# The low part of one product: from a GpSimd subtraction to an adding DMA

## The chip, the core and the metric

The kernel runs on one core of a Trainium2 chip. The metric is the device time of one execution in microseconds (us). Five engines work side by side, each in its own order of instructions, and wait for one another only through semaphores: TensorE (PE in the profile; PEld is its weight load), VectorE (DVE), ScalarE (ACT), GpSimd (POOL) and SyncE (SP, which here only issues DMAs). Sixteen DMA engines move the data.

## The reference

A recommendation model: 32 embedding rows of 64 numbers per sample are looked up, a two-layer "compressed interaction network" is computed on them, and three small dense layers follow. What takes the time is the two interaction layers; all numbers are float32.

```
e   = stack([tbl_f[ids[:, f]] for f in 32 fields], axis=1)        # (1024, 32, 64)
z0  = einsum('bhd,bmd->bhmd', e, e).reshape(batch, 32*32, 64)
o0  = relu(einsum('bcd,oc->bod', z0, W0) + b0)                    # 128 outputs
h   = o0[:, :64]                                                  # 64 go on, 64 are summed
z1  = einsum('bhd,bmd->bhmd', h, e).reshape(batch, 64*32, 64)
o1  = relu(einsum('bcd,oc->bod', z1, W1) + b1)                    # 128 outputs
y   = mlp(concat([sum_d(o0[:, 64:]), sum_d(o1), dense]))
```

## The kernel before, in words

The batch is cut into 128 steps (STEPS) of 8 samples, which give 512 columns (SC = 8 samples x 64 dimensions). In the code m is the step. Fields lie along the 128 partitions. In each step the second layer needs 16 tiles of 128 partitions x 512 columns of products h x e; VectorE makes them in four buffers: p1 (prod[1], 4 tiles), p2 (prod[2], 4 tiles), p3 (prod[3], 4 tiles) and twice 2 tiles in the PSUM buffer z4. A fifth product, prod[0], belongs to the first layer of the next step.

TensorE multiplies plain float32 slowly and a rounded form (float32r) fast. So 14 of the 16 second-layer tiles are split in two: ScalarE writes the rounded part zh (`round_split`, line 372), and somebody writes the rest, zl = product - zh, also in the rounded form. TensorE then makes three fast products for each tile, W1h x zh, W1l x zh and W1h x zl (`split`, line 625). The five parts u are: 0 (4 tiles of p1), 1 (4 tiles of p2), 2 (the first 2 tiles of p3), 3 and 4 (2 tiles each, from z4). The other 2 tiles of p3 go in whole (`whole`, line 616). The low part zl is made by GpSimd for u = 0, 1, 2 (`low_part`, line 217) and by VectorE for u = 3, 4 (`low_part4`, line 512).

The order on each engine is written out by hand, and semaphores of one count per step tie them together. In step m:

- TensorE: split(m-1, 1), split(m-1, 4), split(m-1, 2); first layer of step m+1 (lines 609 and 611); split(m, 3), split(m, 0), the whole tiles. So part 2 of step m is used in TensorE's turn m+1, right ahead of the first layer of step m+2.
- ScalarE: copy_x; in even steps copy_left, in odd ones round_left; round_split 0 and 3; finish_l1(m-1) (line 378), which reads the finished second layer of step m-1 and so waits for split(m-1, 2); round_split 1 and 4; replicate_h0(m+1) (line 385), which waits for the first layer of step m+1; finish_l0(m+1) (line 402); round_split 2; replicate_h1(m+1) (line 385).
- VectorE: product 0 of step m+1, low_part4(m-1, 1), p1, z4, p2, low_part4(m, 0), z4 again, p3, the sum of the second layer of step m-1; every second step three small operations more. The first z4 waits for replicate_h1, low_part4(m, 0) for round_split 3.
- GpSimd: two gathers of embedding rows (line 200), low_part 0, 1, 2, in odd steps the row numbers (line 196).
- SyncE issues all other loads: rot_low for step m+4 and rot_high for step m+2 (1 MB each, line 269), replicated rows, and the write of gathered rows to DRAM (line 259). DMAs issued by GpSimd go to a queue of their own (q0 in the profile), SyncE's to q1.

The semaphores around the change: zh_made[2] is raised by ScalarE's rounding of part 2, zl_made[2] by GpSimd's subtraction; TensorE's split waits for zl_made, and VectorE waits for zl_made[2] of the step before ahead of writing p3 again.

Of the kernel before, what the change touches and what calls it, by code (L numbers as in the profile page):

```python
# [5 lines left out]
F32 = mybir.dt.float32  # L6
F32R = mybir.dt.float32r
I32 = mybir.dt.int32
ALU = mybir.AluOpType
ACT = mybir.ActivationFunctionType  # L10
# [48 lines left out]
SIZES = (4, 4, 2, 2, 2)  # L59
# [6 lines left out]
def cin_mlp(nc, ids, first_row, tables, dense_t, w0_first, w0_second, w0l_first, w0l_second, w1, b0, b1,  # L66
            w_top1, b_top1, w_top2, b_top2, w_top3, y):
    ctx = ExitStack()
    with ctx:
# [6 lines left out]
        def sem(name):  # L76
            return ctx.enter_context(nc.semaphore(name))
# [53 lines left out]
        gather_started = sem("gather_started")  # L131
# [19 lines left out]
        p1_made = sem("p1_made")  # L151
        p2_made = sem("p2_made")
        p3_made = sem("p3_made")
        z4_made = [sem(f"z4_made{k}") for k in range(2)]
        zh_made = [sem(f"zh_made{u}") for u in range(PARTS)]
        zl_made = [sem(f"zl_made{u}") for u in range(PARTS)]
# [32 lines left out]
        def is_up_to(i, c, m):  # L189
            return not known(i) or BODY * i + c <= m  # L190

        @block.gpsimd
        def _(pool):

            def number_rows(n, b):
                pool.tensor_tensor(idx[b][:, :], ids_sb[:, bass.ds(n * GATHERS, GATHERS)], first_row_sb[:, :],  # L196
                                   ALU.add).then_inc(idx_made, 1)

            def gather(b, g):
                pool.indirect_dma_start(  # L200
                    out=emb[b][:, g, :], out_offset=None, in_=tables,
                    in_offset=bass.IndirectOffsetOnAxis(ap=idx[b][:, g:g + 1], axis=0),
                ).then_inc(gathered[b], 16)

            def gathers(i, c):
                n, b = i * 2 + c // 2 + AHEAD, (c // 2 + AHEAD) % 2
                if c % 2 == 0:
                    pool.wait_ge(idx_made, n + 1)
                    pool.sem_inc(gather_started, 1)
                for g in range(c % 2 * 2, c % 2 * 2 + 2):  # L210
                    gather(b, g)

            def low_part(m, u, product):
                pool.wait_ge(zh_made[u], m + 1)
                if not known(m) or m > 0:
                    pool.wait_ge(split_used[u], m)
                pool.tensor_tensor(zl[u][:, :, :], product[:, 0:SIZES[u], :], zh[u][:, :, :].bitcast(F32),  # L217
                                   ALU.subtract).then_inc(zl_made[u], 1)

            def step(i, c):  # L220
                m = i * BODY + c
                if is_up_to(i, c, LAST - 2 * AHEAD):
                    gathers(i, c)
                low_part(m, 0, prod[1])
                low_part(m, 1, prod[2])
                low_part(m, 2, prod[3])
                if c % 2 and is_up_to(i, c, LAST - 2 * AHEAD - 2):
                    n, b = i * 2 + c // 2 + AHEAD + 1, (c // 2 + AHEAD + 1) % 2
                    pool.wait_ge(scratch_written[b], (i + (c // 2 + AHEAD + 1) // 2) * WRITTEN)
                    number_rows(n, b)  # L230

            pool.wait_ge(ids_loaded, 32)
            for n in range(AHEAD):
                if n >= 2:
                    pool.wait_ge(scratch_written[n % 2], WRITTEN)
                number_rows(n, n % 2)
                pool.wait_ge(idx_made, n + 1)
                for g in range(GATHERS):
                    gather(n % 2, g)
            pool.wait_ge(scratch_written[AHEAD % 2], AHEAD // 2 * WRITTEN)  # L240
            number_rows(AHEAD, AHEAD % 2)
            for c in range(BODY):
                step(0, c)
            with pool.Fori(1, ITERS - 2) as i:
                for c in range(BODY):
                    step(i, c)
            for k in (ITERS - 2, ITERS - 1):
                for c in range(BODY):
                    step(k, c)
# [97 lines left out]
        def _(act):  # L347
# [20 lines left out]
            def round_split(m, u, made, product):  # L368
                act.wait_ge(made, m + 1)
                if not known(m) or m > 0:  # L370
                    act.wait_ge(split_used[u], m)
                act.activation(zh[u][:, :, :], product, ACT.Copy).then_inc(zh_made[u], 1)  # L372
# [32 lines left out]
            def step(i, c):  # L405
                m = i * BODY + c
                b = c % HALVES
                if is_up_to(i, c, LAST - 2):
                    copy_x(m + 2, b)
                if b == 0 and is_up_to(i, c, LAST - 2):  # L410
                    copy_left(i * 2 + (c + 2) // 2)
                if b == 1 and is_up_to(i, c, LAST - 1):
                    round_left(i * 2 + (c + 1) // 2)
                round_split(m, 0, p1_made, prod[1][:, :, :])
                round_split(m, 3, z4_made[0], z4[:, :, :])
                if is_past(i, c, 0):
                    finish_l1(m - 1)
                round_split(m, 1, p2_made, prod[2][:, :, :])
                round_split(m, 4, z4_made[1], z4[:, :, :])
                if is_up_to(i, c, LAST - 1):  # L420
                    replicate_h0(m + 1)
                    finish_l0(m + 1, 1 - b, i * 2 + (c + 1) // 2)
                round_split(m, 2, p3_made, prod[3][:, 0:SIZES[2], :])
                if is_up_to(i, c, LAST - 1):
                    replicate_h1(m + 1)

# [58 lines left out]
        def _(dve):  # L485
# [41 lines left out]
            def step(i, c):  # L527
                m = i * BODY + c
                b = c % HALVES
                later = not known(m) or m > 0  # L530
                low = rot_low[c]
                high = rot_high[b]
                if is_up_to(i, c, LAST - 1):
                    products_l0(m + 1, (c + 1) % 4, i + (c + 1) // 4 + 1)
                if later:
                    low_part4(m - 1, 1)
                if b == 1 and is_up_to(i, c, LAST - 1):
                    left_products(i * 2 + (c + 1) // 2)
                dve.wait_ge(hrep0_made, m + 1)
                if later:  # L540
                    dve.wait_ge(zl_made[0], m)
                nc.vector.tensor_tensor(prod[1][:, :, :], repeated(hrep[0], LOW), low[:, :, :],  # L542
                                        ALU.mult).then_inc(p1_made, 1)
                if b == 1 and is_up_to(i, c, LAST - 1):
                    left_low(i * 2 + (c + 1) // 2)
                dve.wait_ge(hrep1_made, m + 1)
                if later:
                    dve.wait_ge(zl_made[4], m)
                nc.vector.tensor_tensor(z4[:, :, :], repeated(hrep[1], 2), low[:, 0:2, :],  # L549
                                        ALU.mult).then_inc(z4_made[0], 1)  # L550
                if b == 1:
                    sum_l0(i * 2 + c // 2)
                dve.wait_ge(rot_high_loaded[b], (i * 2 + c // 2 + 1) * (16 * QUADS))
                if later:
                    dve.wait_ge(zl_made[1], m)
                nc.vector.tensor_tensor(prod[2][:, :, :], repeated(hrep[0], LOW), high[:, :, :],  # L556
                                        ALU.mult).then_inc(p2_made, 1)
                low_part4(m, 0)
                dve.wait_ge(zl_made[3], m + 1)
                nc.vector.tensor_tensor(z4[:, :, :], repeated(hrep[1], 2), low[:, 2:4, :],  # L560
                                        ALU.mult).then_inc(z4_made[1], 1)
                if later:
                    dve.wait_ge(zl_made[2], m)
                    dve.wait_ge(whole3_used, m)
                nc.vector.tensor_tensor(prod[3][:, :, :], repeated(hrep[1], LOW), high[:, :, :],  # L565
                                        ALU.mult).then_inc(p3_made, 1)
                if later:
                    sum_l1(m - 1)
# [32 lines left out]
        def _(pe):  # L601
# [16 lines left out]
                mm.then_inc(used, 1)  # L618

            def split(m, u, start=False, stop=False):  # L620
                pe.wait_ge(zl_made[u], m + 1)
                for t in range(SIZES[u]):
                    k = FIRST[u] + t
                    for part, (w, z) in enumerate(((w1h, zh[u]), (w1l, zh[u]), (w1h, zl[u]))):
                        mm = nc.tensor.matmul(out1[:, :], w[:, k, :], z[:, t, :], start=start and t == 0 and part == 0,  # L625
                                              stop=stop and t == SIZES[u] - 1 and part == 2)
                mm.then_inc(split_used[u], 1)
# [116 lines left out]
```

## Time and profile before

| What | us |
|---|---|
| Median of 3 runs (lowest, highest) | 2021.87 (2021.35, 2022.53) |
| The profiled execution, its own time | 2021.81 |
| Its span in the trace | 2020.0 |
| TensorE busy with matmuls | 1967.9 |
| VectorE busy | 1931.2 |
| GpSimd busy | 1731.4 |
| ScalarE busy | 1679.0 |

The span runs from the first to the last instruction of the trace; the execution's own time holds 1.8 us more. An engine is busy while one of its computing instructions runs; waiting and issuing DMAs don't count. Shares of busy time are means over the whole span; the start and the end take some 85 us, and the rest is the loop of steps, which repeats every two steps.

### The profile page before, as it was taken

To read this page: it belongs to the slowest core of one execution; us is meant where nothing else is said; L and a number is where in the kernel's file an instruction comes from. 1 tells how busy PE (TensorE), PEld (TensorE's weight loads), DVE (VectorE), ACT (ScalarE), POOL (GpSimd) and SP (SyncE) were. 2 spreads that over 40 slices of the span, in tenths; PEclk is the share of its full clock that TensorE was granted. 3 is DMA by queue.
4 is the path that set the end of the run, shared out by engine and by line. 5 is a ranking of instruction groups with operands and counts; after the bars stand their busy time and mean duration, and the time that the engine had idled before them with its cause. 6 is when DMAs were issued, how large, how long until landed. Compare 5 with 4: busy or idle time off the path is not lost.

```text
span 2020.0 us, 28616 instructions
## 1 busy us (share of the span) xinstructions
PE 1967.9 (97%) x7112; PEld 1333.8 (66%) x7112; DVE 1931.2 (96%) x1356; ACT 1679.0 (83%) x1943; POOL 1731.4 (86%) x708
## 2 busy tenths in 40 slices
PE   2999999999999999999999999999999999999998
PEld 0666666666666666666666666666666666666664
DVE  3999999999999999999999999999999999999991
ACT  2888888888888888888888888888888888888883
POOL 3998998998998998998988988988988989988871
PEclk9999999999999999999999999999999999999999
DMA  7998788788788788788888887887888887887820
GB/s 188 207 212 205 176 189 193 177 190 192 178 189 191 181 188 190 182 189 187 184 187 187 185 190 183 186 188 184 187 189 182 188 190 180 190 189 179 190 67 1
DMA packets 268306, 364.14 MB, mean 180 GB/s; under 512 B 107506, under 2 KB 107890, under 8 KB 268163
## 3 DMA queue, kind: packets, MB, share of 16 engines
q1 hardware_dynamic: 258338, 352.61, 77.1%
q0 software_dynamic: 8192, 8.40, 1.5%
q10 hardware_dynamic: 1760, 2.96, 0.5%
q8 instruction: 6, 0.10, 0.0%
q14 instruction: 10, 0.07, 0.0%
HBM read 347.02 MB, written 16.78 MB: 180 GB/s over the span
## 4 chain that ended last, share of the span: by engine, by line
PE 94%; POOL 3%; SPq 1%; issue 1%; DMA 1%; ACT 0%; DVE 0%; POOLq 0%
PE out L625 60%; PE out L609 21%; PE out L616 10%; POOL zl L217 2%; PE out L611 1%; POOL emb L200 1%; SPq L259 0%; PE out L673 0%; DMA fields_dram<-emb 0%; PE hrep L673 0%; SPq L284 0%; SPq L269 0%; DMA first_row_sb<-in_first_row 0%; PE out L666 0%; PE z L666 0%
## 5 line engine op out<-in xcount | busy, mean ns | idle before, releaser
L217 POOL TENSOR_TENSOR zl<-prod,zh 128x2048 fp32r<-128x2048 f32 (+1 forms) x384 | 1476.1, 3869 | 120.5 <-ACT zh L372 69.3
L372 ACT ACTIVATE zh<-prod 128x2048 fp32r<-128x2048 f32 (+1 forms) x384 | 626.2, 1631 | 183.3 <-DVE prod L556 79.0
L625 PE MATMUL out<-zh,w1h 128*128 128x512 f32 x1792 | 745.7, 416 | 11.1 <-DVE zl L512 5.0
L625 PE MATMUL out<-zl,w1h 128*128 128x512 f32 x1792 | 700.4, 391 | 0.0
L625 PE MATMUL out<-zh,w1l 128*128 128x512 f32 x1792 | 699.1, 390 | 0.0
L385 ACT ACTIVATE hrep<-out,b_sb 32x512 f32<-32x512 f32 (+1 forms) x768 | 494.7, 644 | 14.5 <-PE out L611 4.7
L609 PE MATMUL out<-prod,w_sb 128*128 128x512 f32 x1024 | 464.1, 596 | 35.6 <-DVE prod L495 30.6
L625 PEld LDWEIGHTS out<-zh,w1h 128*128 128x128 f32 x1792 | 336.8, 188 | 169.2 <-issue 55.5
L625 PEld LDWEIGHTS out<-zh,w1l 128*128 128x128 f32 x1792 | 337.3, 188 | 83.3 <-issue 16.7
L625 PEld LDWEIGHTS out<-zl,w1h 128*128 128x128 f32 x1792 | 336.7, 188 | 74.2
L609 PEld LDWEIGHTS out<-prod,w_sb 128*128 128x128 f32 x1024 | 194.8, 190 | 232.5 <-issue 222.7
L200 POOL DMA_INDIRECT emb<-in_tables,idx x256 | 244.5, 955 | 103.0 <-POOL idx L196 50.5
L512 DVE TENSOR_TENSOR zl<-z,zh 128x1024 fp32r<-128x1024 f32 x256 | 310.5, 1213 | 6.5 <-ACT zh L372 6.5
L372 ACT ACTIVATE zh<-z 128x1024 fp32r<-128x1024 f32 x256 | 261.6, 1022 | 65.4 <-DVE z L560 60.7
L495 DVE TENSOR_TENSOR prod<-xr,rot_low 128x2048 f32<-128x2048 f32 x128 | 291.9, 2280 | 19.9 <-DMA rot_low<-fields_dram 15.8
L565 DVE TENSOR_TENSOR prod<-hrep,rot_high 128x2048 f32<-128x2048 f32 x128 | 291.8, 2280 | 0.0
L556 DVE TENSOR_TENSOR prod<-hrep,rot_high 128x2048 f32<-128x2048 f32 x128 | 291.8, 2280 | 0.0
L542 DVE TENSOR_TENSOR prod<-hrep,rot_low 128x2048 f32<-128x2048 f32 x128 | 291.8, 2279 | 0.0
L616 PE MATMUL out<-prod,w_sb 128*128 128x512 f32 x512 | 240.3, 591 | 0.0
L560 DVE TENSOR_TENSOR z<-hrep,rot_low 128x1024 f32<-128x1024 f32 x128 | 157.8, 1232 | 4.4
L549 DVE TENSOR_TENSOR z<-hrep,rot_low 128x1024 f32<-128x1024 f32 x128 | 157.0, 1227 | 2.8 <-ACT hrep L385 0.8
L616 PEld LDWEIGHTS out<-prod,w_sb 128*128 128x128 f32 x512 | 96.3, 188 | 71.5 <-issue 61.6
(52 smaller groups left out, 751.1 us busy)
## 6 DMA issues: line engine op xcount, KB each, us to landing
rot_low<-fields_dram SPq DMA_DIRECT2D x512, 256.0 KB
rot_high<-fields_dram SPq DMA_DIRECT2D x512, 256.0 KB
xrep<-fields_dram SPq DMA_DIRECT2D x256, 128.0 KB
fields_dram<-emb SPq DMA_DIRECT2D x512, 32.0 KB
left_x<-fields_dram SPq DMA_DIRECT2D x256, 64.0 KB
left_y<-fields_dram SPq DMA_DIRECT2D x256, 64.0 KB
emb<-in_tables,idx POOLq DMA_INDIRECT x256
w_sb<-in_w ACTq DMA_DIRECT2D x1, 1024.0 KB
```

The costliest lines, as they stand in the source:

```text
L200: pool.indirect_dma_start(out=emb[b][:, g, :], out_offset=None, in_=tables, in_offset=bass.IndirectOffsetOnAxis(ap=idx[b][:, g:g + 1], axi ...
L217: pool.tensor_tensor(zl[u][:, :, :], product[:, 0:SIZES[u], :], zh[u][:, :, :].bitcast(F32), ALU.subtract).then_inc(zl_made[u], 1)
L372: act.activation(zh[u][:, :, :], product, ACT.Copy).then_inc(zh_made[u], 1)
L385: op = act.activation(hrep[j][to, :], out0[h, :], ACT.Relu, bias=b0_sb[h, :])
L495: nc.vector.tensor_tensor(prod[0][:, :, :], repeated(xr, LOW), rot_low[c][:, :, :], ALU.mult).then_inc(x_made, 1)
L512: nc.vector.tensor_tensor(zl[3 + k][:, :, :], z4[:, :, :], zh[3 + k][:, :, :].bitcast(F32), ALU.subtract).then_inc(zl_made[3 + k], 1)
L542: nc.vector.tensor_tensor(prod[1][:, :, :], repeated(hrep[0], LOW), low[:, :, :], ALU.mult).then_inc(p1_made, 1)
L556: nc.vector.tensor_tensor(prod[2][:, :, :], repeated(hrep[0], LOW), high[:, :, :], ALU.mult).then_inc(p2_made, 1)
L565: nc.vector.tensor_tensor(prod[3][:, :, :], repeated(hrep[1], LOW), high[:, :, :], ALU.mult).then_inc(p3_made, 1)
L609: nc.tensor.matmul(out0[:, :], w0_sb[:, t, :], prod[0][:, t, :], start=t == 0, stop=False)
L616: mm = nc.tensor.matmul(out1[:, :], w1_sb[:, tiles.start + t, :], product[:, t, :], start=False, stop=False)
L625: mm = nc.tensor.matmul(out1[:, :], w[:, k, :], z[:, t, :], start=start and t == 0 and part == 0, stop=stop and t == SIZES[u] - 1 and part ...
```

## The change

ScalarE writes minus the rounded part into zl[2], directly after it has written the rounded part. GpSimd then issues one DMA from prod[3] to zl[2] that adds (`accum_op=ALU.add`) and so leaves product - rounded part there: 128 partitions of 4 KB, 0.524 MB. Its subtraction of part 2 is gone. Two semaphores are new: low3_filled (ScalarE to GpSimd, the fill is written) and low3_loaded (the DMA has landed), for which TensorE and VectorE now wait where they waited for zl_made[2].

```diff
                 low_part(m, 0, prod[1])
                 low_part(m, 1, prod[2])
-                low_part(m, 2, prod[3])
+                pool.wait_ge(low3_filled, m + 1)
+                pool.sem_inc(gather_started, 1)
+                pool.dma_start(zl[2][:, :, :].bitcast(F32), prod[3][:, 0:SIZES[2], :],
+                               accum_op=ALU.add).then_inc(low3_loaded, 16)
...
                 round_split(m, 2, p3_made, prod[3][:, 0:SIZES[2], :])
+                act.wait_ge(zh_made[2], m + 1)
+                act.activation(zl[2][:, :, :], zh[2][:, :, :].bitcast(F32), ACT.Copy, scale=-1.0).then_inc(low3_filled, 1)
                 if is_up_to(i, c, LAST - 1):
                     replicate_h1(m + 1)
...
                 if later:
-                    dve.wait_ge(zl_made[2], m)
+                    dve.wait_ge(low3_loaded, m * 16)
                     dve.wait_ge(whole3_used, m)
...
             def split(m, u, start=False, stop=False):
-                pe.wait_ge(zl_made[u], m + 1)
+                if u == 2:
+                    pe.wait_ge(low3_loaded, m * 16 + 16)
+                else:
+                    pe.wait_ge(zl_made[u], m + 1)
```

## Rows read from the trace of the kernel before

**Rows 1.** Busy time by window (start:end): PE, PEld, DVE, ACT, POOL; clock; DMA.
```profile
1000.55:1030.79 30.24, 30.18 (x112) 20.61 (x111) 30.08 (x21) 25.99 (x31) 27.03 (x12) 1.00 0.82 186
500.00:1500.00 1000.00, 997.32 (x3641) 681.73 (x3640) 994.63 (x695) 859.69 (x993) 893.30 (x365) 1.00 0.82 187
```

**Rows 2.** Waits, whole run: total us, times, longest.
```profile
PEld out L625 <- POOL zl L217: 45.1, 120, 1.4
```

**Rows 3.** Chain of waits, one step: start us, duration us, what.
```profile
1002.25 3.43 PE out L609 x8
1005.68 0.23 PE out L611
1005.98 4.34 PE out L625 x18
1010.32 1.72 PE out L616 x4
1012.04 5.49 PE out L625 x24
```

**Rows 4.** Timeline of ScalarE, one step: start us, duration us, instruction.
```profile
1007.13 1.03 ACT L372 ACTIVATE zh<-z 128x1024 fp32r<-128x1024 f32 x1 [0.48 <-DVE z L560]
1008.06 1.30 ACT L385 ACTIVATE hrep<-out,b_sb 64x512 f32<-64x512 f32 x2
1009.38 0.69 ACT L402 ACTIVATE relu<-out,b_sb 64x512 f32<-64x512 f32 x1
1010.09 1.06 ACT L372 ACTIVATE zh<-prod 128x1024 fp32r<-128x1024 f32 x1
1011.18 2.62 ACT L385 ACTIVATE hrep<-out,b_sb 32x512 f32<-32x512 f32 x4
1013.82 0.60 ACT L354 ACTIVATE xr<-xrep 128x512 f32<-128x512 f32 x1
1014.36 0.59 ACT L360 ACTIVATE lz<-left_x 128x512 f32<-128x512 f32 x1
1015.44 1.92 ACT L372 ACTIVATE zh<-prod 128x2048 fp32r<-128x2048 f32 x1 [0.50 <-issue]
1017.26 1.00 ACT L372 ACTIVATE zh<-z 128x1024 fp32r<-128x1024 f32 x1
1018.16 0.68 ACT L378 ACTIVATE relu<-out,b_sb 128x512 f32<-128x512 f32 x1
1018.77 1.91 ACT L372 ACTIVATE zh<-prod 128x2048 fp32r<-128x2048 f32 x1
```

**Rows 5.** Timeline of VectorE, columns as in rows 4.
```profile
1005.87 1.23 DVE L560 TENSOR_TENSOR z<-hrep,rot_low 128x1024 f32<-128x1024 f32 x1
1018.65 1.21 DVE L512 TENSOR_TENSOR zl<-z,zh 128x1024 fp32r<-128x1024 f32 x1
```

**Rows 6.** Groups by line and shape: busy us, mean ns, idle before.
```profile
L217 POOL TENSOR_TENSOR zl<-prod,zh 128x2048 fp32r<-128x2048 f32 x256 | 1173.8, 4597 | 120.5 <-ACT zh L372 69.3 <-issue 51.0
L217 POOL TENSOR_TENSOR zl<-prod,zh 128x1024 fp32r<-128x1024 f32 x128 | 308.7, 2412 | 0.0
```

**Rows 7.** Timeline of GpSimd in the loop.
```profile
1006.73 6.98 POOL L217 TENSOR_TENSOR zl<-prod,zh 128x2048 fp32r<-128x2048 f32 x2 [0.34 <-ACT zh L372]
```

**Rows 8.** Timelines of GpSimd and SyncE's queue at the start.
```profile
9.81 0.94 POOL L200 DMA_INDIRECT emb<-in_tables,idx  x1 [0.30 <-issue]
12.26 5.16 SPq L259 DMA_DIRECT2D fields_dram<-emb  x8
```

**Rows 9.** Busy time by window, columns as in rows 1.
```profile
6.00:7.00 1.00, 0.00 (x0) 0.00 (x0) 0.94 (x4) 0.00 (x0) 0.86 (x1) 1.00 0.98 401
1006.00:1008.00 2.00, 2.00 (x9) 1.66 (x10) 2.00 (x2) 1.52 (x2) 1.67 (x2) 1.00 0.12 35
1012.00:1014.00 2.00, 2.00 (x11) 1.60 (x10) 2.00 (x3) 1.95 (x4) 1.86 (x2) 1.00 1.07 234
```

**Rows 10.** Timeline of TensorE after an idle time, and the window behind it.
```profile
41.72 2.68 PE L609 MATMUL out<-prod,w_sb 128*128 128x512 f32 x3 [4.96 <-ACT hrep L385]
42.00:44.00 2.00, 2.00 (x3) 0.66 (x2) 2.00 (x2) 0.00 (x0) 1.42 (x2) 0.50 1.09 246
```

More of the change, by code:

```diff
@@ L153, in cin_mlp @@
         p3_made = sem("p3_made")
+        low3_filled = sem("low3_filled")
+        low3_loaded = sem("low3_loaded")
         z4_made = [sem(f"z4_made{k}") for k in range(2)]
```

## The prediction

> **What bounds the kernel now.** I read first how busy each engine is in the steady loop. Two steps take 30.24 us, 15.12 a step, and in them TensorE works 30.18 us and VectorE 30.08 [rows 1]; over 1000 us the picture is the same (997 and 995). So two engines are full at once. GpSimd has 27.03 of 30.24 and ScalarE 25.99. Second I read the chain of waits: it stays on TensorE through a whole step, its pieces following each other with at most 0.07 us between [rows 3]. Third the waits: the weight loads waited 45.1 us in 120 times for GpSimd's low parts [rows 2], 0.4 us each. But weight loads run ahead of the matmuls, and the matmuls themselves stand still for only 0.06 us in two steps [rows 1]. The reader should see that taking work from GpSimd can give back almost nothing: if both TensorE's and VectorE's gaps closed, at most 30.24 - 30.08 = 0.16 us for two steps, 10 us in 64 pairs. What the change adds to latency and to ScalarE is the question.
>
> **What it removes.** 128 GpSimd subtractions of 2.41 us [rows 6]. The larger ones, 4.60 us each, are the last thing TensorE needs from GpSimd, for part 1; they are gated by ScalarE's rounding, not by the small one: such a pair starts after GpSimd had run dry for 0.34 us [rows 7]. Gain on the path: 0.
>
> **What it adds to ScalarE.** One pass over 128x1024, SBUF to SBUF. Its nearest row is the rounding of the same shape ahead of it, 1.06 us, next instruction 1.09 later [rows 4]; it waits for that rounding's own semaphore, for which I add 0.05. I take 1.15 us; bounds 0.95 (the step from round to next for the PSUM form, 1007.13 to 1008.06 = 0.93) and 1.3. Queued behind it are replicate_h1, the copies, and round_split 0 and 3. Only 0.49 us of idle stands between the copies' end (1014.36 + 0.59 = 1014.95) and round_split 0 (1015.44), so rounding 3 ends 1.15 - 0.49 = 0.66 us later, at 1018.26 + 0.66 = 1018.92 [rows 4]. VectorE begins its low part of that very result at 1018.65 [rows 5]: it would wait 0.27, with the hand-over about 0.3 us. VectorE has no idle time to win it back. In the other step of the pair VectorE comes to that point later, having three small operations more, so the price is 0.3 us a pair, 64 x 0.3 = 19 us. This alone would give 2021.8 + 19 = 2041. GpSimd's issue (a gather's took 0.94 us [rows 8]) replaces 2.41 us of work; GpSimd stays below its bound.
>
> **What it adds as latency.** Before, part 2 was ready 2.4 us after GpSimd got to it. Now it is fill, issue, transfer, landing. TensorE meets part 2 right ahead of the first layer, and ScalarE makes the next fill only behind that first layer's result. That closes a loop through one step, and I add it up from the end E of split(m, 2):
> - first layer of step m+2: 3.43 + 0.23 = 3.66 us [rows 3];
> - ScalarE: in the same time finish_l1, round_split 1 and 4 (0.61 + 1.91 + 0.93, about 3.5 us from E, so level with the 3.66); then replicate_h0 to the start of replicate_h1, 1011.18 - 1008.06 = 3.12 us, in which round_split 2 of step m+1 is made [rows 4];
> - the fill: 1.15 us;
> - GpSimd issues, the data land: L, counted from the start of the issue;
> - split(m+1, 2): 6 of the 24 matmuls of a 5.49 us piece = 1.37 us [rows 3];
> - three hand-overs between engines at about 0.08 us (VectorE to ScalarE took 0.03, 1007.10 to 1007.13 [rows 4, 5]; a longer one is my estimate for PE and the DMA): 0.25.
>
> Sum 3.66 + 3.12 + 1.15 + 1.37 + 0.25 = 9.55 us, plus L. Before, that loop had GpSimd's 2.4 and no fill, 10.8 of 15.12: harmless. Now it takes the period over as soon as L is above 15.12 - 9.55 = 5.57 us. Below that TensorE merely runs somewhat later against VectorE and nothing is lost. GpSimd's order is no hindrance: it ends low part 1 some 4.6 us after ScalarE's rounding 1 (2.6 us behind E), at E + 7.2, before the fill is there at E + 7.9.
>
> **How long is L?** No row shows an adding DMA, nor any 0.5 MB transfer from GpSimd. Fixed part: a 32 KB gather issued at 9.81 was landed when SyncE went on at 12.26, with the DMAs nearly idle: 2.45 us [rows 8]. Moving part: 0.524 MB. At the best rate in the trace, 401 GB/s for long rows [rows 9], counted once, 1.31 us: L = 3.76, the lower bound. But an add must read the target too, so I count 1.05 MB; and it starts some 8 us behind E, when SyncE has just issued 2 MB of rotations, in a burst where the DMAs are full at 234 GB/s [rows 9]. If the added queue gets as much as the burst carries, 234 GB/s, that is 4.5 us: L = 2.45 + 4.5 = 6.95. If it gets half of it, 9.0 us: L = 11.4, the upper bound. I take L = 7.0, since the transfer does lie in the burst but its 4 KB rows are longer than the loads' 2 KB.
>
> A price that only pages have: the Trainium skill, "DMA: Bandwidth & Descriptors", section "Anatomy of one DMA — SWDGE (gpsimd) path", fits one such transfer by about 2.0 us + bytes/436e3. By it L would be 3.2 us and the loop harmless. "Collectives: The Full Stack", "The bandwidth ceiling: the fold count and why AG ≠ RS ≠ AR", speaks against it: adding halves the rate because two sources are read, not because of the sum. No run here shows either.
>
> **The sum.** Period 9.55 + 7.0 = 16.55 us, 1.43 more than 15.12. Over 127 steps 182 us on the profiled execution's own 2021.8 (the median is 0.06 away): 2203 us. ScalarE's 0.3 us vanish in it, since VectorE then has slack. I cost TensorE's clock at nothing: it is 1.00 through the loop [rows 1]. It fell to 0.50, the 1.2 GHz level, after 4.96 us without work [rows 10]; here the stalls are near 1.5 us a step.
>
> **The rivals.**
> - A. The transfer is in time (L below 5.57) and only ScalarE's pass shows: 2041 us. For it: a lower bound of 3.76 and long rows. Against it: the burst. The skill's fit named above would lead here. Chance 0.14.
> - B. The DMA engines fill up. In two steps they are busy 0.82 of 30.24 = 24.8 us [rows 1]; two transfers of 4.5 us make 33.8, or 16.9 a step: 2021.8 + 127 x 1.78 = 2248, near the forecast by another way; at half the rate, with L = 11.4, the period is 20.95 and the time 2762. For it: bursts already run full. Against: in between (1006 to 1008) the share is 0.12 [rows 9]. Chance of a time above 2450 for either reason: 0.15.
> - C. Not slower: the transfer is in time and ScalarE's pass fits as well. The place is VectorE's low part at 1018.65: it decides at a pass of 0.49 + 0.35 = 0.84 us and L below 5.57. Then 2022 us, or down to 2012 with the gaps of the first paragraph closed. Against it: every row of that shape is near 1 us. Chance 0.10.
> - The forecast, a loop with L between 5.57 and about 8.9 (2022 to 2450 us): 0.61.
>
> **The numbers.** A measurement of this kernel can tell 0.2%, about 4 us. All but rival C is slower: 0.90; within 0.2% 0.07, faster 0.03. The range is 2018 to 2450: it takes in A and C nearly whole and the loop up to L = (2450 - 2022)/127 + 5.57 = 8.9, and leaves about 0.17 out, nearly all above.
>
> **What would show it.** In the changed kernel the weight loads of line 625 wait for the DMA zl<-prod once per step, and the chain of waits goes TensorE, ScalarE, DMA, TensorE, with a period near 16.5 us; VectorE shows idle time ahead of z4, waiting for line 385. From GpSimd's DMA to TensorE's next split should be 7 us. The chain still all on TensorE, with VectorE waiting some 0.3 us for the rounding in every second step, would mean A. A DMA share near 1 without quiet windows would mean B. TensorE's clock under 1.00 in the loop would make all of it wrong, upwards.

## The result, and the profile after

| | us |
|---|---|
| Before, median of 4 runs | 2021.8 (2021.4 to 2022.5) |
| Changed, median of 4 runs | 2469.7 (2467.7 to 2480.2) |
| Ratio | 1.2227, 95% interval 1.2201 to 1.2253 |
| Predicted | 2203, range 2018 to 2450 |

The change costs 448 us, 7.0 us for each of the 64 pairs of steps: a pair now takes 37.2 us in place of 30.24. The way was right; the time lies 20 us above the range, and the forecast had only 40% of the loss. The profiled execution is the longest of the four (2480.2 us, span 2478.3). Of all executions here one of the two of the control e8 was disturbed, at a clock of 0.75 and 2850.6 us, and is left out.

The first view is the page of the changed kernel: the busy times, TensorE's granted clock in 40 slices, and the DMA queues (packets, MB, share of 16 engines).

```profile
PE 2145.2 (87%) x7112; PEld 1426.2 (58%) x7112; DVE 1951.1 (79%) x1356; ACT 1812.3 (73%) x2071; POOL 1569.8 (63%) x708
PEclk9998988989989989889889889889899889899899
q1 hardware_dynamic: 258338, 352.61, 61.8%
q0 software_dynamic: 26624, 75.52, 15.8%
```

VectorE's busy time is nearly the old one in a longer span, so it now waits. TensorE has the same 7112 matmuls and is busy 177 us longer: it runs slower, which the clock row, mostly 8 and 9, hints at. The loop's window answers to [rows 1] (columns as there):

```profile
500.00:1500.00 1000.00, 878.87 (x2925) 588.32 (x2926) 807.18 (x559) 745.93 (x850) 652.84 (x292) 0.91 0.80 178
```

No engine is full now, and neither are the DMAs. What is waited for is in the view of the waits, beside [rows 2]:

```profile
ACT relu L383 <- PE out L635: 375.4, 128, 6.4
PE out L635 <- DMA zl<-prod: 285.3, 67, 5.5
POOL zl L230 <- ACT zl L430: 255.1, 122, 3.0
DVE prod L502 <- PE out L618: 233.1, 64, 4.0
DVE left_parts L512 <- ACT left_parts L371: 107.3, 64, 1.7
```

TensorE's matmuls stood still for the adding DMA 285 us in 67 waits (the loop has 64 pairs): in every second step only, 4.3 us each. The chain of waits through one pair, without its smallest pieces, shows the loop (start us, duration us, what):

```profile
1195.94 1.23 DVE z L556
...
1197.89 2.20 DVE prod L563
1200.09 1.14 DVE zl L519
1201.26 1.24 DVE z L567
...
1204.78 0.69 ACT relu L407
1205.49 1.07 ACT zh L377
1206.58 1.06 ACT zl L430
...
1208.23 8.34 DMA zl<-prod
1216.62 2.93 PE out L635 x6
1219.55 4.98 PE out L616 x8
...
1232.26 0.52 ACT left_parts L371
...
1233.53 1.23 DVE z L556
```

From the issue at 1208.23 the data take 8.34 us. Then TensorE makes part 2 in 2.93 us, where six of the 24 matmuls took 1.37, and the first layer in 4.98 where it took 3.43 [rows 3]. ScalarE goes on, and the next fill is there at 1229; but that step's DMA is not on the chain. The chain leaves the even step over round_left, VectorE's small subtraction and z4, and comes to the next odd step's DMA. The reason for the slow matmuls is in the windows of two us (columns as in rows 1; the number before the last two is the clock):

```profile
1212.00:1214.00 2.00, 0.10 (x1) 0.00 (x0) 2.00 (x1) 2.00 (x2) 1.26 (x2) 1.00 1.17 226
1214.00:1216.00 2.00, 0.00 (x0) 0.00 (x0) 1.90 (x3) 0.16 (x1) 2.00 (x1) 0.92 1.03 206
1216.00:1218.00 2.00, 1.38 (x3) 1.16 (x4) 2.00 (x2) 0.00 (x0) 1.86 (x1) 0.50 0.40 91
1220.00:1222.00 2.00, 2.00 (x4) 0.78 (x3) 0.69 (x1) 2.00 (x3) 0.00 (x0) 0.50 1.06 258
1224.00:1226.00 2.00, 2.00 (x10) 1.46 (x9) 1.15 (x1) 1.20 (x2) 2.00 (x1) 1.00 1.06 230
```

After 4.5 us without a matmul TensorE comes back at 0.50 of full speed, its 1.2 GHz level, and has 1.00 again only at about 1224. (1.56 + 1.55 =) 3.1 us are lost to it in this pair.

Where the 8.34 us go is in the queues' packets (queue: packets, MB, share of 16 engines). From 1210 to 1212, two to four us after the issue, only SyncE's queue moves anything, its rotation loads:

```profile
q1 hardware_dynamic: 255, 0.46, 107.2%
```

From 1214 to 1216 nearly all traffic is the adding DMA's own:

```profile
q0 software_dynamic: 119, 0.37, 89.3%
q1 hardware_dynamic: 177, 0.04, 13.6%
```

So the transfer isn't slowed by the burst so much as held back by it. The trace records every packet; medians over steps 9 to 117, counted from the issue, are these. In odd steps the first packet of the adding DMA starts after 4.5 us, when all but a few packets of the rotation loads are through, the last one ends after 7.9, and the landing is at 8.3. In even steps, where SyncE's loads are through before the issue, they are 1.5, 4.4 and 4.7 us. The same transfer is 3.6 us later in odd steps, and 2.9 of them pass before its first packet.

### The profile page after: what moved, and what is told of

It is laid out like the page before. It is cut to its first block, busy times and chain, and to the rows that moved or that the text cites. A ratio compares the mean times of both kernels' runs of the same rounds, so it can differ in the third digit from the quotient of the medians.

```text
span 2478.3 us, 28985 instructions
## 1 busy us (share of the span) xinstructions
PE 2145.2 (87%) x7112; PEld 1426.2 (58%) x7112; DVE 1951.1 (79%) x1356; ACT 1812.3 (73%) x2071; POOL 1569.8 (63%) x708
## 3 DMA queue, kind: packets, MB, share of 16 engines
q0 software_dynamic: 26624, 75.52, 15.8%
## 4 chain that ended last, share of the span: by engine, by line
PE 23%; DMA 23%; ACT 22%; DVE 16%; issue 14%; SPq 1%; DVEq 0%; POOL 0%; POOLq 0%; ACTq 0%
DMA zl<-prod 22%; PE out L616 13%; PE out L635 8%; ACT hrep L390 7%; ACT zh L377 6%; DVE prod L563 5%; ACT relu L407 3%; ACT zl L430 3%; DVE z L567 3%; DVE z L556 3%; DVE zl L519 3%; DVE sums L524 2%; ACT xr L359 1%; ACT left_parts L371 1%; PE out L618 1%
## 5 line engine op out<-in xcount | busy, mean ns | idle before, releaser
L219 POOL TENSOR_TENSOR zl<-prod,zh 128x2048 fp32r<-128x2048 f32 x256 | 1171.2, 4575 | 461.2 <-ACT zh L377 461.2
L635 PE MATMUL out<-zh,w1h 128*128 128x512 f32 x1792 | 794.5, 443 | 292.0 <-DMA zl<-prod 285.3
L635 PE MATMUL out<-zl,w1h 128*128 128x512 f32 x1792 | 731.3, 408 | 0.0
L635 PE MATMUL out<-zh,w1l 128*128 128x512 f32 x1792 | 730.0, 407 | 0.0
L616 PE MATMUL out<-prod,w_sb 128*128 128x512 f32 x1024 | 556.6, 694 | 35.7 <-DVE prod L502 30.7
L635 PEld LDWEIGHTS out<-zh,w1l 128*128 128x128 f32 x1792 | 355.6, 198 | 99.3 <-issue 30.4
L616 PEld LDWEIGHTS out<-prod,w_sb 128*128 128x128 f32 x1024 | 238.2, 233 | 297.8 <-issue 280.8
L383 ACT ACTIVATE relu<-out,b_sb 128x512 f32<-128x512 f32 x128 | 87.9, 687 | 375.4 <-PE out L635 375.4
L230 POOL DMA_DIRECT2D zl<-prod x128 | 124.4, 972 | 269.4 <-ACT zl L430 255.1
L623 PE MATMUL out<-prod,w_sb 128*128 128x512 f32 x512 | 240.3, 591 | 0.0
L530 DVE TENSOR_REDUCE feat<-relu 128x512 f32 (+1 forms) x128 | 87.2, 681 | 98.7 <-ACT relu L383 98.7
```

The costliest lines, as they stand in the source:

```text
L616: nc.tensor.matmul(out0[:, :], w0_sb[:, t, :], prod[0][:, t, :], start=t == 0, stop=False)
L623: mm = nc.tensor.matmul(out1[:, :], w1_sb[:, tiles.start + t, :], product[:, t, :], start=False, stop=False)
```

## The experiments

Three theories stood against each other: the DMA's time to landing closes a loop (the prediction's), with the clock on top; ScalarE's pass costs; the DMAs' traffic costs. Intervals are those of the ratio to the kernel before; "landing" is read from the chain of waits, in odd steps, of which the fences show one each (start us, duration us, what).

**ScalarE's pass alone** (e1).

```diff
# the kernel before, and:
+                act.wait_ge(zh_made[2], m + 1)
+                act.activation(spare[:, :, :], zh[2][:, :, :].bitcast(F32), ACT.Copy, scale=-1.0)
```

> The kernel before, with ScalarE's extra pass of 128x1024 written into a spare tile that nobody reads; GpSimd still subtracts. Theory (the DMA's time from issue to landing closes a loop TensorE, ScalarE, DMA, TensorE; ScalarE's pass is minor): the pass delays rounding 3 in every second step by some 0.3 us, 64 x 0.3 = 19 us, so about 2041 us, at most 2050. Rival 1 (ScalarE's pass is what costs, since it sits ahead of replicate_h1 and round_left): 2200 us or more.

Measured 2035.1 us, ratio 1.0070 (1.0053 to 1.0087): 14 us, of the 19 reckoned. VectorE runs on with 992 of 1000 us busy. The pass is not what costs.

**The same arithmetic, added by GpSimd** (e2).

```diff
-                pool.dma_start(zl[2][:, :, :].bitcast(F32), prod[3][:, 0:SIZES[2], :],
-                               accum_op=ALU.add).then_inc(low3_loaded, 16)
+                pool.tensor_tensor(zl[2][:, :, :], prod[3][:, 0:SIZES[2], :], zl[2][:, :, :].bitcast(F32),
+                                   ALU.add).then_inc(low3_loaded, 16)
```

> The changed kernel, but GpSimd adds the product on to the filled tile by its own instruction (2.4 us) where the changed kernel issues the DMA; all waits as changed. Theory: the loop is 9.55 + about 2.5 = 12 us and does not bind; only ScalarE's pass shows, about 2041 us as in the run with the pass alone. Rival 1 (the pass and its wait cost): as slow as the changed kernel, near 2470. If this is 2041 and the changed kernel 2470, the DMA alone holds some 430 us.

Measured 2038.4 us, ratio 1.0090 (1.0073 to 1.0107). So 431 us of the 448 come with the DMA. GpSimd's own time is not the reason: it is busy 1733 us here against 1570 in the changed kernel. Whether the reason is the DMA's time to landing or its traffic, e4 to e12 tell.

**A plain copy** (e3; the low part is the whole product).

```diff
-                pool.dma_start(zl[2][:, :, :].bitcast(F32), prod[3][:, 0:SIZES[2], :],
-                               accum_op=ALU.add).then_inc(low3_loaded, 16)
+                pool.dma_start(zl[2][:, :, :].bitcast(F32), prod[3][:, 0:SIZES[2], :]).then_inc(low3_loaded, 16)
```

> The changed kernel, but the DMA copies the product over the filled tile instead of adding (the low part is then the whole product; same bytes written, the target not read). Theory with the adding itself costly: the time to landing falls from a median of 6.3 us by 1 to 2 us, the loop by as much, and TensorE's idle times get short enough for its clock to stay up: 2150 to 2300 us. Rival 2 (an add costs what a copy costs; waiting behind the other queue's traffic and the fixed time are what is long): within 30 us of 2470.

Measured 2352.5 us, ratio 1.1640 (1.1621 to 1.1660), 50 us above the expected band but far from the rival. The landing is near 7.0 us in odd steps, 1.3 less than adding, and 2.9 in even ones, where adding takes 4.7:

```profile
1218.54 7.09 DMA zl<-prod
1225.68 2.93 PE out L634 x6
1228.61 5.06 PE out L615 x8
```

TensorE's clock falls here too, so little of its loss comes back. What adding costs the DMA engines is in the queue's share: 

```profile
q0 software_dynamic: 26624, 75.52, 9.0%
```

9.0% of 16 engines over 2350.6 us is 3385 us; the gathers' part is 1.8% of 2035.7 x 16 = 586 (in e2, where the queue has them alone); the rest over 128 x 16 is 1.37 us a transfer and engine. For adding it is 15.8% of 2478.3 x 16 less the same, 2.77 us. Twice the time for the same bytes: 0.524 MB / 2.77 us = 189 GB/s against 383. The Trainium skill ("Collectives: The Full Stack", section "The bandwidth ceiling: the fold count and why AG ≠ RS ≠ AR") says of ring collectives on several cores that the step that adds runs at about half the rate of the one that copies, because an add reads two sources. The ratio of 2.0 agrees with that; that the second read is the reason no run here shows.

**A small adding DMA** (e4; 64 of 1024 columns get the sum).

```diff
-                pool.dma_start(zl[2][:, :, :].bitcast(F32), prod[3][:, 0:SIZES[2], :],
+                pool.dma_start(zl[2][:, 0, 0:64].bitcast(F32), prod[3][:, 0, 0:64],
```

> The changed kernel, but the adding DMA covers 64 of the 1024 columns (32 KB in place of 512 KB; the rest of the low part stays minus the rounded part). Theory (moving bytes is most of the time to landing): landing at about 2.5 to 3.5 us as the gather at the start of the trace before, loop under 13 us, so 2041 us. Rival 2 (the time is queueing behind the other queue's packets, whatever the size): landing stays at 5 us or more and the time above 2150 us.

Measured 2272.9 us, ratio 1.1243 (1.1221 to 1.1266). Here my theory failed: with a sixteenth of the bytes the landing is still near 6.1 us:

```profile
1211.06 5.93 DMA zl<-prod
1217.03 2.87 PE out L635 x6
1219.90 3.82 PE out L616 x8
```

and the queues show why. From 1214 to 1215, over three us after the issue, there is still no packet of GpSimd's queue q0:

```profile
q1 hardware_dynamic: 130, 0.23, 102.7%
```

Its packets come from 1215 to 1216:

```profile
q1 hardware_dynamic: 487, 0.16, 98.4%
q0 software_dynamic: 107, 0.03, 29.0%
```

The first starts 4.3 us after the issue in odd steps (median) and 1.5 us in even ones, as with 512 KB; the last ends 1.2 us later. Bytes are the smaller part of the landing; most of it is the wait for the first packet, and that is there for 32 KB too. The Trainium skill ("DMA: Bandwidth & Descriptors", "Queues, rings and completion order") has each DMA engine take turns between the queues that have work, a packet (there a group of descriptors) at a time, by which so small a transfer should have passed the burst early. The long start does not look like it. What follows does: from 1214 to 1215 in the changed kernel q0 and q1 have 48 packets each.

**TensorE kept busy in the stall** (e5; w_zero is a tile of zeros, so the sum is unchanged).

```diff
                     split(m - 1, 4)
+                    if c % 2 == 0:
+                        for _ in range(18):
+                            nc.tensor.matmul(out1[:, :], w_zero[:, :], w1h[:, 0:4, :], start=False, stop=False)
                     split(m - 1, 2, stop=True)
```

> The changed kernel, with 18 extra matmuls by a tile of zeros (they add nothing to the sum) in every second step, between split(m-1, 4) and split(m-1, 2), where TensorE stands still for 4.5 to 5 us until the DMA has landed. They are some 4.1 us of work at 2.4 GHz. Theory (the stall makes the clock fall to 0.50, and the matmuls behind it cost 3.1 us more in every second step: 2.93 in place of 1.37 for split 2, 4.98 in place of 3.43 for the first layer): the clock stays near 1.00 and the kernel gets faster although it does more, 64 x 3.1 = 200 us, so about 2270 us. Rival (the clock is no part of it, the landing alone is): no change, 2470, or slower by the added work.

Measured 2316.7 us, ratio 1.1455 (1.1436 to 1.1474): 153 us faster than the changed kernel, with 1152 matmuls more. The landing is what it was, the matmuls behind it are quick:

```profile
1201.29 8.20 DMA zl<-prod
1209.54 1.66 PE out L639 x6
1211.19 3.43 PE out L620 x8
```

The clock over the loop is 1.00, and a pair takes 34.8 us in the trace in place of 37.5. So at least 153 us, a third of the 448, was the clock's fall. The control, the same 18 matmuls in the kernel before (e8):

> Control for the zero matmuls: the kernel before with the same 18 in every second step. There TensorE has no idle time, so 18 x 0.228 = 4.1 us a pair should show in full: 2021 + 64 x 4.1 = 2284 us. If they cost much less, they are no measure of work.

Measured 2260.9 us in one run: 240 us, 3.7 a pair. The added matmuls are real work, which only the stall hides.

**SyncE's loads behind the landing** (e6).

```diff
                     sp.wait_ge(z4_made[1], m + 1)
+                    sp.wait_ge(low3_loaded, m * 16 + 16)
                     load_low(m + 4, c)
```

> The changed kernel, but SyncE issues a step's rotation loads and writes to DRAM only after that step's adding DMA has landed, so that it doesn't meet the burst that they make. Theory (the long landings, 8.3 us in odd steps, last until the other queue's burst is over): landing falls to the 4.7 us of the shortest ones or somewhat over, TensorE's stalls and the clock's fall go, 2040 to 2150 us. Rival (the landing time is the DMA's own): landing stays at 6 to 8 us, 2470 us or more, since loads now come later too.

Measured 2183.2 us (2166.6 to 2193.0), ratio 1.0773 (1.0725 to 1.0822), somewhat over the band. Not a byte less is moved, and 287 us are gone. The first packet starts 2.2 us after the issue, and the landing is 5.2 to 6.1 us in most odd steps:

```profile
1200.73 5.97 DMA zl<-prod
1206.75 2.21 PE out L636 x6
1208.96 4.53 PE out L617 x8
```

**A quarter of the rotation bytes in the loop** (e9).

```diff
+                few = 1 if not known(m) else LOW
-                                  ap=[[PITCH, FIELDS], [QUADS * PITCH, LOW], [1, SC]])
-                    sp.dma_start(tile[q * FIELDS:(q + 1) * FIELDS, :, :], src).then_inc(loaded, 16)
+                                  ap=[[PITCH, FIELDS], [QUADS * PITCH, few], [1, SC]])
+                    sp.dma_start(tile[q * FIELDS:(q + 1) * FIELDS, 0:few, :], src).then_inc(loaded, 16)
```

> The changed kernel, but the rotation loads inside the loop fetch one of four rows (a quarter of the bytes, the rest of the tiles keeps old values). Theory (queueing behind the burst): the DMA lands in 4.7 us or less in all steps, 2040 to 2060 us. Rival (its own time, or one-way effects of ScalarE's pass): landing above 6 us and more than 2300 us.

Measured 2131.2 us, ratio 1.0538 (1.0520 to 1.0555). The first packet starts after 1.5 us in odd steps too. The landing is steady at 5.05 us, but that is still too long; both sides' bands missed.

```profile
1198.95 5.05 DMA zl<-prod
1204.05 1.65 PE out L636 x6
1205.70 3.43 PE out L617 x8
```

The next odd DMA is issued at 1230.45 there: a pair of 31.50 us, of which 26.45 is everything but the landing. The same for e5: 34.85 - 8.25 = 26.6, taking the pair as 30.24 + (2316.7 - 2021.8)/64 and the landing's usual 8.25. So the loop is about 26.5 us plus the landing in one of two steps, and binds from a landing of 30.24 - 26.5 = 3.7 us on.

**Both small** (e12: the diffs of e4 and e9 together).

> The changed kernel with both a quarter of the rotation bytes and an adding DMA of 32 KB. With the three other cases (full and small DMA beside full loads, full DMA beside light loads) it gives the landing's parts. Theory: floor of 2.5 to 3.5 us from issue to landing; the loop 29 to 30 us, under 30.24, so only ScalarE's pass shows: 2035 to 2045 us. Rival (a fixed time over 4 us even for a small adding DMA with quiet DMAs): 2060 us or more.

Measured 2054.5 us, ratio 1.0164 (1.0147 to 1.0181), between the two bands and 16 us over e2. TensorE waited for the DMA 6 times in all, 13.4 us, of which 13.0 near the start and the end, where the loads are full; so the loop no longer binds. Most landings are missing from this trace, but the DMA's last packet ends 2.0 to 2.2 us after the issue in odd and even steps alike. A long fixed time, the rival, is not what e4 met.

**ScalarE's round_left earlier** (e10).

```diff
-                if b == 1 and is_up_to(i, c, LAST - 1):
-                    round_left(i * 2 + (c + 1) // 2)
...
                 act.activation(zl[2][:, :, :], ..., scale=-1.0).then_inc(low3_filled, 1)
+                if b == 0 and is_up_to(i, c, LAST - 2):
+                    round_left(i * 2 + (c + 2) // 2)
```

> The changed kernel, with ScalarE's round_left moved from the start of an odd step to the end of the even step before, ahead of replicate_h1 (4 copies, 2.62 us) and copy_x. Theory as it now stands (the loop runs over two steps: DMA in the odd one, TensorE, ScalarE, round_left, VectorE's small subtraction and z4, p2, ScalarE, DMA; its length is 26.3 us + the landing + the clock's loss): VectorE no longer waits 1.7 us for round_left, z4 starts when replicate_h1 ends, 1.3 us earlier than now; 64 x 1.3 = 83 us, so about 2385 us. Rival (the loop goes through one step, TensorE, ScalarE, DMA, as predicted, and VectorE isn't in it): no change, 2470.

Measured 2475.2 us, ratio 1.2251 (1.2230 to 1.2271): nothing gained. This is not the rival's one-step loop either. Its chain of waits:

```profile
1200.99 9.71 DMA zl<-prod
1210.75 2.93 PE out L635 x6
1213.67 4.82 PE out L616 x8
...
1218.73 4.13 PE out L635 x18
1222.86 1.72 PE out L623 x4
1224.57 5.49 PE out L635 x24
1230.06 3.43 PE out L616 x8
...
1238.57 9.60 DMA zl<-prod
```

round_left and VectorE are off the chain, as meant; the even step now goes through TensorE's own work. The loop without the landing fell to (37.58 - 9.71 =) 27.9 us, clock loss included, from 37.59 - 8.34 = 29.2 (z4 to z4, 1195.94 to 1233.53). But the landing grew from 8.34 to 9.71, the same 1.4 us. Why is in SyncE's order: the step's first rotation loads, in the changed kernel and here, are issued at

```profile
1202.67 1.87 SPq L274 DMA_DIRECT2D rot_low<-fields_dram  x4
1197.12 1.95 SPq L274 DMA_DIRECT2D rot_low<-fields_dram  x4
```

The adding DMA follows 5.6 us behind them there and only 3.9 here, and its first packet comes after 5.6 us (median) in place of 4.5. From these loads to the landing it is 13.9 us there and 13.6 here, and from the landing to the next odd step's rotation loads (1240.26 and 1234.33) 23.7 and 23.6. z4, which releases them, was ready at 1195.25 here, but SyncE was still issuing the loads of left_y until 1196.9. So the DMA issued earlier lands no earlier. The reader should see that an edit can be right about the path and still gain nothing, if what it brings forward then waits for something that the edit did not move.

**round_left earlier and loads behind the landing** (e11: the diffs of e6 and e10 together).

> The same together with SyncE's loads behind the landed DMA, the two changes that shorten the loop without taking away work. Theory: 2183 less up to 83 us, so 2080 to 2120 us; it stays above the kernel before, since the loop's 25 us and a landing near 6 still exceed 30.24. Rival: 2183, as with the loads alone.

Measured 2172.8 us, ratio 1.0751 (1.0733 to 1.0769): 10 us less than e6 alone, which is within the spread of e6's runs, and not the 60 to 100 forecast. The landings are 6.1 to 7.0 us in most odd steps against 5.2 to 6.1 in e6, and the first packet starts after 3.0 us in place of 2.2: as in e10, most of what the path over round_left gives is spent on a longer landing. No version here beats the kernel before: the best that keeps the DMA and all the work is this one, 151 us above it.

## Why the prediction was wrong

What bounds the kernel before: right as far as the runs go. TensorE is full: 18 matmuls more cost 3.7 us a pair (e8). That relieving GpSimd gives nothing is read from the rows; no run tests it without the other parts of the change, and no version is under 2035.

ScalarE's pass: right. 19 us forecast, 14.0 measured alone (e1), 17 with GpSimd adding (e2).

The mechanism, a loop TensorE, ScalarE, fill, DMA, TensorE that takes the period over: right in kind. From the odd DMA's issue to the even one's (1229.59 in the changed kernel's timeline of GpSimd) it took 21.36 us; the prediction's sum 9.55 with the measured landing 8.34 and the clock's 3.1 gives 21.0. One hand-over was set too short: the fill ends at 1206.58 + 1.06 = 1207.64 and GpSimd's DMA begins at 1208.23, 0.6 us later and not 0.08. But the loop was drawn through one step and taken for both alike. It binds in odd steps; the even one takes 16.2 us, held by what lies between its fill and the next odd one, with no DMA on the chain; that this is near the forecast's 16.55 is chance. For a pair the prediction had 2 x 16.55 = 33.1 us, the changed kernel 37.2.

The landing: 7.0 forecast, 8.3 measured in odd steps (8.1 to 8.6 in four of five). Mis-sized by 1.3 us in the step that counts, 64 x 1.3 = 83 us. Its makeup was wrong too. A fixed 2.45 and bytes at the burst's rate would have made e4's 32 KB land in under 3 us; it took 6.1. What holds it is the other queue's burst, shown by e6 (the same bytes, moved behind: 5.2 to 6.1) and e9 (fewer of them: 5.05), and the adding itself 1.3 (e3). The forecast had the transfer share the burst's rate for 4.5 us; in the trace it waits 2.9 us longer than in even steps for its first packet and then has the engines nearly alone, for 3.4 us. That 7.0 came near 8.3 is in part luck. The transfer should have been read against when the rotation loads ahead of it are through, not against the burst's rate.

The step that failed: "I cost TensorE's clock at nothing", with its reason "here the stalls are near 1.5 us a step". I had spread the loop's excess evenly over the steps. It comes in one stall of 4.5 us in every second step, and behind that the clock is at 0.50 for some 7 us. By the trace's matmuls 3.1 us a pair, by e5 at least 153 us of the total, 2.7 us a pair in the loop, which is the difference between 2470 and 2317. With the clock held the time lies inside the range, 114 us over the point. I had named a clock under 1.00 as what would make all of it wrong, and gave it no price and no chance, though [rows 10] showed the fall.

The rivals: A (in time, only ScalarE's pass) needed a landing under 5.57; the loop as measured needs 3.7, and even with light loads it was 5.05. C the same. B (DMA engines full) is not what happened: their share over the loop is 0.80 against 0.82, and after the burst there are windows at 0.00. The Trainium skill's fit for one transfer from GpSimd ("DMA: Bandwidth & Descriptors", "Anatomy of one DMA — SWDGE (gpsimd) path"), 3.2 us for 0.5 MB, is met by the plain copy in its even steps (2.9 us, e3), and missed by every adding DMA (4.7 in even steps, 5.05 with light loads) and by every landing beside the burst; that fit says nothing of adding or of a second queue.

What stays open: why GpSimd's packets start only when the rotation loads are nearly through. It is shown that they do (the changed kernel, e4, e10), and that no single late engine is the cause: none of the 16 has a packet of it before, and their 16 increments of the semaphore come within 0.8 us (median). Whether the engines take what SyncE queued first, or the DMA's descriptors reach them late, no run tells apart. And how the 250 us that the DMA still cost in e4 divide between its stall and the clock was not tried apart.

## What to carry to other kernels

A DMA in place of a late instruction is priced by when it lands in the worst phase of the other queues' traffic, not by its bytes: ask what was queued ahead of it and when that is through. If that makes TensorE wait, add up the wait per stall and not per step on average, since one stall of 4.5 us halved the clock for the matmuls behind it; the added zero matmuls of e5, which made the kernel 153 us faster, are a quick test for that share. And before moving work off an engine that isn't full, add up the idle time of the full ones: here it was 0.16 us a pair, and no more could come back.

## What the runs showed of the hardware that was not expected

- An adding DMA of 0.524 MB within SBUF takes the DMA engines 2.77 us, a plain one 1.37; to issue, GpSimd needs 0.97 against 0.58 us.
- Behind 2 MB of rotation loads in SyncE's queue an adding DMA from GpSimd moved its first packet 4.3 to 4.5 us after the issue, with 32 KB as with 512 KB, and 1.5 us after it where the loads were through. So 32 KB took 6.1 us to land.
- Between the end of ScalarE's fill and the start of GpSimd's DMA instruction lay 0.6 us, where GpSimd's subtractions began within 0.1 of their rounding. A semaphore increment by GpSimd stands ahead of the DMA; its share was not tried apart.
- TensorE's clock was 0.50 from the first matmul after 4.5 us of idle time, for about 7 us of work; with matmuls of zeros in the gap it stayed at 1.00.
